# Linear attention and a soft tree on one core: the order of the fills, the residual in quarters, and where normalising, the state and the output's norm stand on VectorE

## The chip, the cores and the metric

The kernel runs on one core of a Trainium2 chip. The metric is the device time of one execution in microseconds (us), the median of the runs. TensorE, VectorE, ScalarE, GpSimd (POOL in the profile) and SyncE (SP) each work through a list of instructions of their own and meet only at semaphores.

## What is computed

x is [4, 2048, 256] in f32. Each row is normalised, xn = (x - mean)/sqrt(var + 1e-5), and the output is x + attention(xn) + tree(xn).

```python
# attention: 16 heads of 64
Q = phi(xn @ Wq + bq);  K = phi(xn @ Wk + bk);  V = xn @ Wv + bv      # phi(a) = elu(a) + 1
KV = KV + k_i v_i^T;  Ks = Ks + k_i                                   # token by token
o_i = (q_i KV) / (q_i Ks + 1e-6);   attention = o @ Wo + bo
# tree of depth 8
gate = sigmoid((xn @ tree_Wq^T) @ routers^T)
leaf_prob = product of gate or 1 - gate along each of 256 paths
tree = (leaf_prob @ leaf_values) @ Wout_w^T + Wout_b
```

## The kernel before

**Blocks, units, fills.** The 8192 tokens are worked in 16 blocks g of 512 (4 blocks a sequence), and a block in 8 units p, one for each pair of heads; n = 8g + p counts the units. The scan is done in chunks of 64 tokens. A unit has on TensorE first a *tiled* part (`tiled`, lines 974 to 994) of 64x64 matmuls: queries n on the state (`from_state`, in two passes), outer products of keys and values of unit n+1, queries on the state again, the scores of unit n+1 (line 893), then the chunk products of unit n with the masked scores (line 947). After it come the *fills*: each fill writes one bank of PSUM.

Matrix products in f32 are made of three passes over high and low halves, so a K, Q or V fill is six matmuls of 512 columns (`split_product`, line 806; the matmuls all have line 811). Unit n fills K of unit n+3, Q of unit n+2, and pieces of other work: V0 and V1 (values for heads 0 to 7 and 8 to 15, four chunks of 128 tokens each), xT (a transpose of the normalised x of block g+1), leaf (a transpose of the leaf probabilities), gate (the tree's gates of block g+1). The last unit of a block has oT (a transpose of the attention output) and y (the two output products, line 826).

**What sets the order.** `unit_fills` (lines 39 to 70) writes it by hand: K in bank W0, the "head" in S1, Q in S0, the "tail" in W1. All engines follow this one list; the banks S0 and S1 are also where the scores go. So a unit's scores wait (line 970 and 971) until the Q fill of the unit before has been converted and S0 and S1 are drained. `until_drained` in `outer_products` makes unit 0 wait for all four V0 chunks and unit 4 for all four V1 chunks.

In the loops over units each engine has a fixed sequence:

- ScalarE (lines 599 to 625): copies the scores out of PSUM (line 562, `copy_scores`), puts the transposed output of unit n-1 together (line 552), then for each fill relu and exp of K or Q (lines 522, 525), high halves of xT, leaf, oT (515, 545), tanh of the gates (530). The high half of the turned output (558) comes behind Q.
- VectorE (lines 765 to 794): `norm` (703 to 709: denominator, reciprocal, product) of unit n, `carry` (732: the running state, eight additions) of unit n+1, in unit 0 `normalise` (645) of the next block, then for each fill the drain: phi of K or Q (659), values (668), low halves (651, 683). `values_first` puts V ahead of Q in units 2 and 6 on VectorE alone. The low half of the turned output (697) comes last. `layer_norm` (632, 635) of block g+2 is in unit 7, and so are the outputs y (690).
- GpSimd (lines 478 to 504): the mask of the scores (406), the copy that takes the output apart into 16-bit planes (459), the copy that puts the turned keys together (467), the copy that takes the new keys apart (449), in unit 1 the `residual` (414: x plus bias into y_buf, for the whole block), in unit 7 the tree levels (422 to 439), and in unit 0 `inverse_deviation` (388, 390).
- SyncE: `turn_output` and `turn_keys` (DMA transpositions, lines 346 and 334), the stores of the block before in unit 0, and the load of block g+2 in unit 2, behind that unit's two transpositions.

TensorE's queue is kept short of waits: those that a unit needs are put ahead of the last matmul of a fill (`at_last`), where the matmuls before it still run: `head_ready` in K, `normed` (the output of unit n is out of PSUM) in Q, `masked` (the scores of n+1 are masked) in the last V.

## Time and profile before

| | us |
|---|---|
| median of 3 runs | 1218.85 (1218.16 to 1219.29) |
| the profiled execution, its own time | 1219.74 |
| its span (first to last instruction) | 1218.0 |
| TensorE matmuls busy | 1161.8 (95%) |
| VectorE busy | 836.1 (69%) |
| GpSimd busy | 804.3 (66%) |
| ScalarE busy | 681.0 (56%) |
| mean granted TensorE clock | 0.997 of full speed |

"Busy" is the time in which at least one instruction of the engine ran. A view of waits or of the timeline adds in brackets how long the engine had been idle ahead of an instruction and what released it. Matmuls overlap, so each is listed with more time than the distance to the next; distances are read from starts.

### The profile page before, as it was taken

What the parts mean: (1) busy time and instruction counts of PE and PEld (TensorE: products, weight loads), DVE (VectorE), ACT (ScalarE), POOL (GpSimd) and SP (SyncE); (2) the same over time, 40 slices, a digit from 0 to 9 for tenths busy, and PEclk for the clock granted to TensorE, in tenths of its full rate; (3) what the DMA queues carried; (4) which work ended last, traced back from release to release, by engine and by line L of the source; (5) the groups of instructions that cost most, each with busy time, mean ns of one, the idle gap of its engine ahead of it and who ended that gap; (6) DMA issues with size and microseconds to landing.
All of it is one profiled execution on the core that took longest, in us unless ns stands there. A gap on an engine that the chain in (4) does not pass through costs nothing.

```text
span 1218.0 us, 48108 instructions
## 1 busy us (share of the span) xinstructions
PE 1161.8 (95%) x21233; PEld 996.0 (82%) x21233; DVE 836.1 (69%) x2186; ACT 681.0 (56%) x990; POOL 804.3 (66%) x951
## 2 busy tenths in 40 slices
PE   5899999999999999999999999999999999999986
PEld 4789788887878879778897888878788797888866
DVE  4775875858677585876858667585876758767482
ACT  3563674737557374673737547374673746647371
POOL 3586667667666676766667676676666667676571
PEclk9999999999999999999999999999999999999998
DMA  7143532525344252533524435252452625335251
GB/s 233 20 80 52 86 68 54 91 52 89 60 65 90 45 97 50 89 63 55 93 49 90 58 62 98 45 89 54 84 68 57 94 45 89 63 57 77 55 71 36
DMA packets 271298, 87.54 MB, mean 72 GB/s; under 512 B 250721, under 2 KB 269424, under 8 KB 271088
## 3 DMA queue, kind: packets, MB, share of 16 engines
q1 hardware_dynamic: 271088, 84.46, 39.0%
q8 instruction: 166, 2.72, 1.0%
q14 instruction: 44, 0.36, 0.1%
HBM read 14.43 MB, written 8.39 MB: 19 GB/s over the span
## 4 chain that ended last, share of the span: by engine, by line
PE 63%; DVE 18%; ACT 6%; DMA 5%; issue 4%; POOL 3%; SPq 1%; POOLq 0%; ACTq 0%; DVEq 0%
PE w_pair L811 17%; PE s_pair L811 11%; PE s_pair L826 9%; PE o_pair L826 9%; PE s_pair L893 5%; PE o_pair L947 4%; DVE snaps L732 4%; DVE qT L659 3%; PE o_pair L933 3%; DVE oT L697 3%; DVE v_aug L668 3%; DVE xn L645 2%; DMA k_turned<-k_planes 2%; PE kv_pair L906 2%; ACT ex L522 2%
## 5 line engine op out<-in xcount | busy, mean ns | idle before, releaser
L406 POOL TENSOR_SCALAR_AFFINE_SELECT aT<-aT 64x512 f32<-64x512 f32 x256 | 171.7, 671 | 264.6 <-ACT aT L562 254.9
L562 ACT ACTIVATE aT<-s_pair 128x512 f32<-128x512 f32 x128 | 76.5, 598 | 382.6 <-PE s_pair L893 382.6
L811 PE MATMUL w_pair<-xnT,wk 128*128 128x512 f32 x768 | 212.1, 411 | 2.2 <-ACT k_tok L535 2.2
L811 PE MATMUL s_pair<-xnT,wq 128*128 128x512 f32 x756 | 201.1, 401 | 0.6 <-DVE o_tok L709 0.3
L732 DVE TENSOR_TENSOR snaps<-kv_pair,snaps 128x65 f32<-128x65 f32 x768 | 173.4, 226 | 26.4
L467 POOL COPY k_tok<-k_turned 128x1024 uint16<-128x1024 uint16 x126 | 171.4, 1361 | 22.7 <-POOL ffn_tok L459 14.6
L811 PE MATMUL w_pair<-wv,xnT 128*128 128x512 f32 x654 | 170.0, 395 | 0.0
L525 ACT ACTIVATE ex<-ex 128x512 f32<-128x512 f32 x256 | 161.9, 633 | 8.1
L449 POOL COPY k_planes<-kT 128x1024 uint16<-128x1024 uint16 x126 | 132.7, 1053 | 49.2 <-issue 26.5
L811 PEld LDWEIGHTS w_pair<-xnT,wk 128*128 128x128 f32 x768 | 134.3, 188 | 34.4 <-ACT k_tok L535 2.7
L811 PEld LDWEIGHTS s_pair<-xnT,wq 128*128 128x128 f32 x756 | 135.1, 188 | 27.0 <-DVE o_tok L709 2.4
L811 PEld LDWEIGHTS w_pair<-wv,xnT 128*128 128x128 f32 x654 | 122.8, 188 | 28.5
L659 DVE SCALAR_TENSOR_TENSOR qT<-s_pair,bias_one,ex 128x512 f32<-128x512 f32 x126 | 94.1, 747 | 61.2 <-ACT ex L525 61.2
L459 POOL COPY ffn_tok<-o_tok 128x1024 uint16<-128x1024 uint16 x109 | 113.5, 1041 | 7.6 <-DMA ffn_tok<-ffn_tok 0.8
L522 ACT ACTIVATE ex<-w_pair,neg_bias 128x512 f32<-128x512 f32 x130 | 89.6, 689 | 48.0 <-PE w_pair L811 47.2
L933 PE MATMUL o_pair<-snaps,qT 64*64 64x65 f32 x3584 | 113.5, 224 | 0.5 <-DVE state L732 0.4
L522 ACT ACTIVATE ex<-s_pair,neg_bias 128x512 f32<-128x512 f32 x126 | 86.8, 689 | 48.0 <-PE s_pair L811 47.6
L906 PE MATMUL kv_pair<-v_aug,k_tok 64*64 64x65 f32 x4096 | 92.1, 220 | 14.4 <-POOL k_tok L467 8.6
L697 DVE TENSOR_TENSOR oT<-o_full,oT 128x512 fp32r<-128x512 f32 x109 | 99.3, 911 | 3.0 <-ACT oT L558 3.0
L659 DVE SCALAR_TENSOR_TENSOR kT<-w_pair,bias_one,ex 128x512 f32<-128x512 f32 x128 | 95.2, 744 | 8.1 <-ACT ex L525 5.2
L826 PE MATMUL o_pair<-wo,oT 128*128 128x256 f32 x768 | 98.7, 283 | 1.8 <-DVE oT L697 1.8
L893 PE MATMUL s_pair<-qT,kT 64*64 64x64 f32 x4096 | 87.0, 221 | 12.2 <-DVE qT L659 9.0
(117 smaller groups left out, 2076.6 us busy)
## 6 DMA issues: line engine op xcount, KB each, us to landing
x_in<-in_L_attn_x_dram SPq DMA_DIRECT2D x16, 256.0 KB, 3.1
x_in<-in_L_attn_x_dram SPq DMA_DIRECT2D x32, 128.0 KB, 3.2
out_dram<-y_buf SPq DMA_DIRECT2D x32, 128.0 KB, 1.7
out_dram<-y_buf SPq DMA_DIRECT2D x64, 64.0 KB, 2.3
k_turned<-k_planes SPq DMA_TRANSPOSE x126, 3.2
stage<-in_L_attn_Wv_dram SPq DMA_DIRECT2D x2, 512.0 KB, 7.8
stage<-in_L_attn_Wk_dram SPq DMA_DIRECT2D x2, 512.0 KB, 10.0
stage<-in_L_attn_Wq_dram SPq DMA_DIRECT2D x2, 512.0 KB, 12.2
```

The lines of the kernel that those rows point to most:

```text
L406: pool.affine_select(out=part, in_=part, compare_op=ALU.is_ge, fill=0.0, base=0, pattern=[[0, 2 * CH], [1, D]], channel_multiplier=-1).the ...
L449: pool.tensor_copy(k_planes[:, :, :], kT[:, m % 2].bitcast(U16).rearrange("p (t s) -> p s t", s=2))\
L467: pool.tensor_copy(k_tok[:, :, :].rearrange("p c f -> p (c f)").bitcast(U16) .rearrange("p (n s) -> p s n", s=2), k_turned[:, :, :].rearra ...
L522: act.activation(ex[:, slot], psum_of(name), ACT.Relu, scale=-1.0, bias=neg_bias[:, col:col + 1])\
L525: act.activation(ex[:, slot], ex[:, slot], ACT.Exp, scale=-1.0).then_inc(exp_ready, 1)
L659: dve.scalar_tensor_tensor(out=dst, in0=psum_of(name), scalar=bias_one[:, col:col + 1], in1=ex[:, slot], op0=ALU.add, op1=ALU.max)\
L697: dve.tensor_tensor(oT[:, 1, p], o_full[:, 1, p], oT[:, 0, p].bitcast(F32), ALU.subtract)\
L732: dve.tensor_tensor(dst, added, so_far, ALU.add).then_inc(sum_ready, 1)
L811: last = pe.matmul(dst, l, r, start=i == 0, stop=i == len(steps) - 1)
L826: last = pe.matmul(dst[:, (c % 2) * hid:(c % 2 + 1) * hid], oT[:, a, t, tile_of_output(c)] if t < PAIRS else leafT[:, a, t - PAIRS, cols], ...
L893: last = pe.matmul(s_pair[rows_of(a), h, t * D:(t + 1) * D], kT[rows_of(h), p % 2, at], qT[rows_of(h), p % 2, at], start=True, stop=True)
L933: last = pe.matmul(output_at(t, h, a), qT[rows_of(h), p % 2, t * P + a * D:t * P + (a + 1) * D], before, start=turn == 0 and half not in b ...
```

## The change

- The fills of a unit become K, V, Q, and then what is left. V1's chunks 2 and 3 go from the tail to the head in units 1 and 2, V0's four chunks of the next block from the tail to the head in units 3 to 6; xT, leaf and gate go to the tail, behind Q.
- VectorE's order in a unit becomes: carry of unit n+1, norm of unit n, K, V, low half of the turned output, Q, tail. `values_first` goes. ScalarE's high half of the turned output comes right behind K.
- `normalise` of block g+2 stands in unit 7 of block g, behind `layer_norm`, instead of in unit 0 of block g+1; GpSimd's `inverse_deviation` for it goes between two tree levels. It has a new wait for the put-together outputs that lie in the same buffer.
- The residual is made in four parts, in units 1, 3, 4 and 5; the load of block g+2 moves from unit 2 to unit 6 on SyncE.
- TensorE's waits move: masks at the half of Q, norm at its last matmul, xT drained at the last matmul of K, the tail's needs at the last matmul of V.

```diff
@@ -42,19 +42,20 @@
     keys = divmod(n + 3, PAIRS) if n + 3 < blocks * PAIRS else None
     queries = divmod(n + 2, PAIRS) if n + 2 < blocks * PAIRS else None
     more = g + 1 < blocks
+
     head, tail = [], []
     if p == 0:
         head, tail = [("V1", 0, g)], [("V1", 1, g)]
     if p in (1, 2):
-        tail = [("V1", p + 1, g)]
+        head = [("V1", p + 1, g)]
         if more:
-            head = [("xT", p - 1, g + 1)]
+            tail = [("xT", p - 1, g + 1)]
+    if 3 <= p < PAIRS - 1 and more:
+        head = [("V0", p - 3, g + 1)]
     if p in (3, 4):
-        head = [("leaf", p - 3, g)]
-        if more:
-            tail = [("V0", p - 3, g + 1)]
+        tail = [("leaf", p - 3, g)]
     if p in (5, 6) and more:
-        head, tail = [("gate", p - 5, g + 1)], [("V0", p - 3, g + 1)]
+        tail = [("gate", p - 5, g + 1)]
     fills = [(("K", keys[1], keys[0]), W0)] if keys else []
@@ -363,8 +364,8 @@
                     turn_output(n)
                 if n + 3 < UNITS:
                     turn_keys(n + 3)
-                if p == 2 and g + 2 < BLOCKS:
-                    sp.wait_ge(x_consumed, g + 1)
+                if p == 6 and g + 2 < BLOCKS:
+                    sp.wait_ge(x_consumed, CH * (g + 1))
                     load_block(g + 2)
             store(BLOCKS - 1)
             sp.wait_ge(y_stored, STORES * BLOCKS)
@@ -407,13 +408,12 @@
                                        pattern=[[0, 2 * CH], [1, D]], channel_multiplier=-1).then_inc(a_masked, 1)
                 pool.wait_ge(a_masked, 2 * n + 2)
-            def residual(g):
+            def residual(g, c):
                 if g:
                     pool.wait_ge(y_stored, STORES * g)
                 pool.wait_ge(x_loaded[g % 2], LOADS * (g // 2 + 1))
-                pool.tensor_tensor(y_buf[:, :, :], x_in[:, g % 2],
-                                   y_bias[:, 0].unsqueeze(1).to_broadcast([P, CH, hid]), ALU.add)\
-                    .then_inc(x_consumed, 1)
+                pool.tensor_tensor(y_buf[:, c], x_in[:, g % 2, c], y_bias[:, 0], ALU.add).then_inc(x_consumed, 1)
+                pool.wait_ge(x_consumed, CH * g + c + 1)
             def gates(g):
                 for i in range(2):
@@ -438,6 +438,7 @@
                 pool.wait_ge(leaf_step, g * LEVEL_STEPS + 2 * l + 2)
                 pool.tensor_tensor(left, src[:, :, 0:n], right, ALU.subtract).then_inc(leaf_step, 1)
+            RESIDUAL_AT = (1, 3, 4, 5)
             FIRST_LEVELS = {0: range(0, 5), 1: range(5, 7), 2: range(7, depth)}
             def take_apart(m):
@@ -477,9 +478,9 @@
             take_apart(2)
             for n in range(UNITS):
                 g, p = divmod(n, PAIRS)
-                if p == 0 and g + 1 < BLOCKS:
-                    inverse_deviation(g + 1)
-                    pool.wait_ge(rstd_ready, 2 * g + 4)
+                if n == 0:
+                    inverse_deviation(1)
+                    pool.wait_ge(rstd_ready, 4)
                 if n + 1 < UNITS:
                     mask(n + 1)
                 if by_dma(n):
@@ -488,9 +489,8 @@
                     put_together(n + 2)
                 if n + 3 < UNITS:
                     take_apart(n + 3)
-                if p == 1:
-                    residual(g)
-                    pool.wait_ge(x_consumed, g + 1)
+                if p in RESIDUAL_AT:
+                    residual(g, RESIDUAL_AT.index(p))
                 if n in FIRST_LEVELS:
                     for l in FIRST_LEVELS[n]:
                         level(l, 0)
@@ -500,6 +500,10 @@
                     pool.wait_ge(o_turned_in, 16 * units_by_dma(n))
                     for l in range(depth):
+                        if l == 4 and g + 2 < BLOCKS:
+
+                            inverse_deviation(g + 2)
+                            pool.wait_ge(rstd_ready, 2 * g + 6)
                         level(l, g + 1)
                     pool.wait_ge(leaf_step, (g + 2) * LEVEL_STEPS)
@@ -605,15 +609,12 @@
                     put_output_together(n - 1)
                 for name, _ in unit_fills(n // PAIRS, n % PAIRS, BLOCKS):
                     kind, i, g = name
+                    if turned and kind != "K":
+                        high_of_turned(n - 1)
+                        turned = False
                     if kind in "KQ":
                         exponential(name)
-                        if kind == "Q" and turned:
-                            high_of_turned(n - 1)
-                            turned = False
                     elif kind == "oT":
-                        if turned:
-                            high_of_turned(n - 1)
-                            turned = False
                         high_of_output(name)
                     elif kind == "xT":
                         high(name, xnT[:, g % 2, 0, i])
@@ -641,6 +642,9 @@
                 if g == 1:
                     dve.wait_ge(filled[bank_of["tree", 1, 0]], count_of["tree", 1, 0])
+                if g > 1:
+
+                    dve.wait_ge(o_whole, units_by_dma((g - 1) * PAIRS - 2))
                 for c in range(CH):
                     last = dve.tensor_scalar(xn[:, c], x_in[:, g % 2, c], mean_var[:, c, 0:1], rstd[:, c:c + 1],
                                              ALU.subtract, ALU.mult)
@@ -669,14 +673,6 @@
                                   bv_all[:, half * n:(half + 1) * n].rearrange("p (h e) -> p h e", e=D), ALU.add)\
                    .then_inc(drained[bank_of[name]], 1)
-            def values_first(fills, p):
-
-                if p not in (2, PAIRS - 2):
-                    return fills
-                return [f for f in fills if f[0] not in ("Q", "V0", "V1", "oT", "kT")] + \
-                    [f for f in fills if f[0] in ("V0", "V1")] + \
-                    [f for f in fills if f[0] in ("Q", "oT", "kT")]
-
             def low_of_output(name):
                 _, p, g = name
                 dve.wait_ge(oT_hi, g * PAIRS + p + 1)
@@ -685,7 +681,7 @@
             def output(name):
                 i = name[1]
-                dve.wait_ge(x_consumed, name[2] + 1)
+                dve.wait_ge(x_consumed, CH * (name[2] + 1))
                 dve.wait_ge(filled[bank_of[name]], count_of[name])
                 dve.tensor_tensor(y_buf[:, 2 * i:2 * i + 2], psum_of(name).rearrange("p (c d) -> p c d", d=hid),
                                   y_buf[:, 2 * i:2 * i + 2], ALU.add)\
@@ -764,24 +760,24 @@
             for n in range(UNITS):
                 g, p = divmod(n, PAIRS)
-                norm(n)
                 if n + 1 < UNITS:
                     carry(n + 1)
-                if p == 0 and g + 1 < BLOCKS:
-                    normalise(g + 1)
-                fills = [name for name, _ in unit_fills(g, p, BLOCKS)]
+                norm(n)
+                if n == 0:
+                    normalise(1)
                 turned = n and by_dma(n - 1)
-                for name in values_first(fills, p):
+                for name, _ in unit_fills(g, p, BLOCKS):
                     kind, i, b = name
+                    if turned and kind not in ("K", "V0", "V1"):
+                        low_of_turned(n - 1)
+                        turned = False
                     if kind in "KQ":
                         phi(name)
                     elif kind == "oT":
-                        if turned:
-                            low_of_turned(n - 1)
-                            turned = False
                         low_of_output(name)
                         if p == PAIRS - 1 and g + 2 < BLOCKS:
                             layer_norm(g + 2)
+                            normalise(g + 2)
                     elif kind in ("V0", "V1"):
                         values(name)
                     elif kind == "xT":
@@ -803,9 +799,11 @@
                     waited[id(signal)] = count
                     pe.wait_ge(signal, count)
-            def split_product(dst, lhs, rhs, tiles, at_last=None):
+            def split_product(dst, lhs, rhs, tiles, at_half=None, at_last=None):
                 steps = [s for t in range(tiles) for s in passes(lambda a, t=t: lhs(a, t), lambda a, t=t: rhs(a, t))]
                 for i, (l, r) in enumerate(steps):
+                    if at_half and i == len(steps) // 2:
+                        at_half()
                     if at_last and i == len(steps) - 1:
                         at_last()
                     last = pe.matmul(dst, l, r, start=i == 0, stop=i == len(steps) - 1)
@@ -834,7 +832,7 @@
                 at = c % 2 * (CH // 2) + c // 2
                 return slice(at * P, (at + 1) * P)
-            def fill(name, at_last=None):
+            def fill(name, at_half=None, at_last=None):
                 kind, i, g = name
                 bank, dst = bank_of[name], psum_of(name)
@@ -843,11 +841,11 @@
                 if kind in "KQ":
                     wt = wk if kind == "K" else wq
                     last = split_product(dst, lambda a, t: wt[:, a, t, i * P:(i + 1) * P],
-                                         lambda a, t: xnT[:, g % 2, a, t], KT_, at_last)
+                                         lambda a, t: xnT[:, g % 2, a, t], KT_, at_half, at_last)
                 elif kind in ("V0", "V1"):
                     half, n = int(kind[1]), 2 * HALF * D
                     last = split_product(dst, lambda a, t: xnT[:, g % 2, a, t, i * P:(i + 1) * P],
-                                         lambda a, t: wv[:, a, t, half * n:(half + 1) * n], KT_, at_last)
+                                         lambda a, t: wv[:, a, t, half * n:(half + 1) * n], KT_, at_half, at_last)
                 elif kind in ("xT", "leaf"):
                     src = xn if kind == "xT" else leaf_even
                     for c in range(CH):
@@ -1051,13 +1049,18 @@
                 def normed():
                     until(o_normed, n + 1)
-                def head_ready():
-
+                def tail_ready():
                     for kind, i, g in (f for f, _ in fills):
                         if kind == "xT":
                             until(xn_ready, g + 1)
-                        if kind == "leaf" and i == 0:
+                        if kind == "leaf":
                             until(leaf_step, (g + 1) * LEVEL_STEPS)
+
+                def inputs_ready():
+                    for kind, i, g in (f for f, _ in fills):
+                        if kind == "V0" and i == 0:
+                            for t in range(KT_):
+                                until_drained(("xT", t, g))
                 def masked():
                     if n + 1 < UNITS:
@@ -1069,18 +1072,20 @@
                         until(s_copied, n + 2)
                     if kind in ("oT", "y"):
                         normed()
-                    if kind == "V0" and i == 0:
-                        for t in range(KT_):
-                            until_drained(("xT", t, g))
                     if kind == "leaf":
-                        until(leaf_step, (g + 1) * LEVEL_STEPS)
+                        tail_ready()
                     if kind == "y" and i == 0:
                         for t in range(LT):
                             until_drained(("leaf", t, g))
-                    fill(name, head_ready if kind == "K" else normed if kind == "Q" else masked if bank == W1 and kind in ("V0", "V1") else None)
-                    if kind == "y" and i == 0:
-                        masked()
+                    if kind == "K":
+                        fill(name, at_last=inputs_ready)
+                    elif kind == "Q":
+                        fill(name, masked, normed)
+                    elif kind in ("V0", "V1"):
+                        fill(name, at_last=tail_ready)
+                    else:
+                        fill(name)
                 normed()
                 masked()
```

## Rows read from the trace of the kernel before

**Rows 1.** The page, busy time, share of the span and instructions.

```profile
PE 1161.8 (95%) x21233; PEld 996.0 (82%) x21233; DVE 836.1 (69%) x2186; ACT 681.0 (56%) x990; POOL 804.3 (66%) x951
```

**Rows 2.** Timeline, ScalarE, line 562: start, duration (us), instruction, idle time and its releaser.

```profile
120.53 0.60 ACT L562 ACTIVATE aT<-s_pair 128x512 f32<-128x512 f32 x1 [13.73 <-PE s_pair L893]
...
413.49 0.60 ACT L562 ACTIVATE aT<-s_pair 128x512 f32<-128x512 f32 x1 [13.74 <-PE s_pair L893]
421.95 0.60 ACT L562 ACTIVATE aT<-s_pair 128x512 f32<-128x512 f32 x1 [2.30 <-PE s_pair L893]
428.79 0.60 ACT L562 ACTIVATE aT<-s_pair 128x512 f32<-128x512 f32 x1 [1.11 <-PE s_pair L893]
437.03 0.60 ACT L562 ACTIVATE aT<-s_pair 128x512 f32<-128x512 f32 x1 [2.52 <-PE s_pair L893]
...
450.71 0.60 ACT L562 ACTIVATE aT<-s_pair 128x512 f32<-128x512 f32 x1 [1.11 <-PE s_pair L893]
458.48 0.60 ACT L562 ACTIVATE aT<-s_pair 128x512 f32<-128x512 f32 x1 [1.11 <-PE s_pair L893]
466.82 0.60 ACT L562 ACTIVATE aT<-s_pair 128x512 f32<-128x512 f32 x1 [1.69 <-PE s_pair L893]
486.32 0.60 ACT L562 ACTIVATE aT<-s_pair 128x512 f32<-128x512 f32 x1 [13.74 <-PE s_pair L893]
...
1148.66 0.60 ACT L562 ACTIVATE aT<-s_pair 128x512 f32<-128x512 f32 x1 [14.61 <-PE s_pair L893]
1156.46 0.60 ACT L562 ACTIVATE aT<-s_pair 128x512 f32<-128x512 f32 x1 [1.63 <-PE s_pair L893]
```

**Rows 3.** Timeline, VectorE, block 5, unit 0: normalising.

```profile
416.96 2.26 DVE L645 TENSOR_SCALAR xn<-x_in,mean_var,rstd 128x256 f32<-128x256 f32 x4
```

**Rows 4.** Timeline, block 5, start of unit 3: the last V1 chunk and TensorE.

```profile
434.88 0.68 DVE L668 TENSOR_TENSOR v_aug<-w_pair,bv_all 128x512 f32<-128x512 f32 x1
435.61 0.34 PE L906 MATMUL kv_pair<-v_aug,k_tok 64*64 64x65 f32 x8 [0.51 <-DVE v_aug L668]
```

**Rows 5.** Residual and low half, block 5, unit 2; then line 697 alone: min/median/max ns.

```profile
427.79 2.38 POOL L414 TENSOR_TENSOR y_buf<-x_in,y_bias 128x1024 f32<-128x1024 f32 x1
428.45 2.26 DVE L697 TENSOR_TENSOR oT<-o_full,oT 128x512 fp32r<-128x512 f32 x1
...
L697 DVE TENSOR_TENSOR oT<-o_full,oT x109: 678/682/2827, 84.6 to 1200.5; 128x512 fp32r<-128x512 f32 x109
```

**Rows 6.** Timeline, TensorE, block 5, unit 0: outer products, scores, Q fill.

```profile
412.08 0.65 PE L906 MATMUL kv_pair<-v_aug,k_tok 64*64 64x65 f32 x32
412.78 0.65 PE L893 MATMUL s_pair<-qT,kT 64*64 64x64 f32 x32
...
416.72 1.55 PE L811 MATMUL s_pair<-xnT,wq 128*128 128x512 f32 x6
```

**Rows 7.** Timeline, block 15, units 4 to 5: Q filled last, then the scores.

```profile
1180.22 1.08 PE L811 MATMUL s_pair<-xnT,wq 128*128 128x512 f32 x4
...
1181.34 0.69 ACT L522 ACTIVATE ex<-s_pair,neg_bias 128x512 f32<-128x512 f32 x1
1182.72 0.75 DVE L659 SCALAR_TENSOR_TENSOR qT<-s_pair,bias_one,ex 128x512 f32<-128x512 f32 x1 [0.48 <-ACT ex L525]
...
1183.53 0.69 PE L893 MATMUL s_pair<-qT,kT 64*64 64x64 f32 x32 [0.44 <-DVE qT L659]
```

**Rows 8.** Timeline, VectorE, block 5, unit 0: first of norm, first of carry.

```profile
413.96 0.17 DVE L703 TENSOR_SCALAR den<-o_pair 128x8 f32<-128x8 f32 x1 [1.29 <-PE o_pair L947]
...
415.01 0.22 DVE L732 TENSOR_TENSOR snaps<-kv_pair,state 128x65 f32<-128x65 f32 x1
```

**Rows 9.** The page, groups: count, busy us, mean ns, idle us before and releaser.

```profile
L467 POOL COPY k_tok<-k_turned 128x1024 uint16<-128x1024 uint16 x126 | 171.4, 1361 | 22.7 <-POOL ffn_tok L459 14.6
...
L449 POOL COPY k_planes<-kT 128x1024 uint16<-128x1024 uint16 x126 | 132.7, 1053 | 49.2 <-issue 26.5
```

**Rows 10.** The page, DMA issues: count, size, median us from issue to landing.

```profile
x_in<-in_L_attn_x_dram SPq DMA_DIRECT2D x32, 128.0 KB, 3.2
```

## The prediction

> **What bounds the kernel now.** I read the page first: TensorE is busy for 1161.8 of 1218.0 us [rows 1], so time goes only where TensorE works or waits, and a gain must be a wait taken away. Next I read the copies of the scores on ScalarE (line 562). Each starts 0.71 us after TensorE's scores begin, so they are a clock of the units. In block 5 [rows 2] the copies are 8.46, 6.84, 8.24, 13.68 (two of 6.84), 7.77, 8.34 and 19.50 us apart, for units p = 0 to 7: 72.83 in all. I count each interval from the scores inside unit p to those inside unit p+1, and it holds p's fills. The mean over blocks 1 to 14 is (1148.66 - 120.53)/14 = 73.44 [rows 2].
>
> What would be the length without waits? Units 1 to 4 hold the same fills (K, Q, V and a transpose) and three of them take 6.84, so 2 is 1.40 too long. Units 5 and 6 hold K, Q, V and gate: 7.77 against 8.34, 0.57 too long. Unit 0 takes 7.80 in the last block (1148.66 to 1156.46), where nothing is normalised, against 8.46: 0.66 too long. 7.80 + 4 x 6.84 + 2 x 7.77 + 19.50 = 70.20. So block 5 waits 2.63 us and the mean block 3.24 us; over 15 blocks some 48 us, 4% of the span, is all that an order of work can win.
>
> The timeline names the causes. (a) Unit 0: VectorE spends 2.26 us on normalising at 416.96, its queue is late, and TensorE waits for Q [rows 3]. (b) Unit 2: the last V1 chunk is filled last, is drained at 434.88 to 435.56, and the outer products of the next unit wait 0.51 us for it; that V is also ahead of Q on VectorE [rows 4]. (c) Unit 6 the same with V0 of the next block. (d) In unit 2 the residual also holds GpSimd for 2.38 us from 427.79; VectorE's low half of the turned output starts at 428.45 and takes 2.26 us instead of 0.68, ending 0.54 after the residual does [rows 5].
>
> **What the change costs and gives.** *Removed.* V goes ahead of Q, so the last V1 or V0 is drained most of a unit before its outer products: (b) and (c) go. Normalising goes to unit 7 of the block before, where TensorE has 19.50 us of its own work: (a) goes. The residual in quarters is about 2.38/4 = 0.6 us a piece (a fixed part would make it more; 0.74 would still fit) and no longer holds VectorE for long: (d) goes. I count all 3.24 us of a mean block as won. If a third of what the mean has over block 5 (0.61) stays, it is 0.2 us a block.
>
> *Added: Q is late.* This is the step that decides. At present in units 1 to 4 a V fill follows Q before TensorE comes to the next scores. In the changed kernel only a transpose of four matmuls does. The scores need Q converted: ScalarE's two passes and VectorE's one. The length of that loop stands in the trace. Unit 0 already has the order K, V, Q: scores start at 412.78, Q's last matmul ends at 416.72 + 1.55 = 418.27, which is 5.49 us [rows 6]. From the end of Q to the scores that wait for it: in the last block Q is filled right before the next unit. It ends at 1180.22 + 1.08 = 1181.30, ScalarE begins at 1181.34, VectorE's pass ends at 1183.47, and the scores start at 1183.53 after an idle time put down to it: 2.23 us [rows 7]. The loop is 5.49 + 2.23 = 7.72, and 0.04 more because scores that have waited take 0.69 instead of 0.65: 7.76. TensorE's own work is 6.84. So each interval of units 1 to 4 grows to 7.76, a new wait of 0.92 (0.88 without the slower restart). Units 0, 5 and 6 have 1.4 us of fill behind Q both before and after: 7.80 and 7.77, just above the loop.
>
> A mean block becomes 7.80 + 4 x 7.76 + 2 x 7.77 + 19.50 = 73.88 against 73.44: +0.44, times 14 = **+6.2 us**.
>
> *Block 0.* Units 3 and 4 gain a wait of 0.92 each, unit 6 gives 0.57 back. In units 1 and 2 the output is transposed by TensorE on S1, and its low half now stands behind the transpose of x on both ScalarE and VectorE; nothing shows this order. It lies between nothing and about 1 us a unit (a ScalarE and a VectorE pass of some 0.5 each more); I take 1, since no fill is left behind it to cover it. Sum 1.84 - 0.57 + 2 = **+3.3** (1.3 at the low end). *Last block.* There is no V0, x or gate, so Q stands directly before the next unit in units 1 and 2: about 1 us each lost; in the last units carry is started without waiting for the end of the chunk products, which gives about as much back. I take 0, from -2 to +2.
>
> *State before output on VectorE.* Carry takes 416.96 - 415.01 = 1.95 us and norm 415.01 - 413.96 = 1.05 [rows 3, 8]. Carry needs only the outer products and both state passes, so it starts earlier, but the output is normed 1.95 - 0.9 = about 1.1 us later in an open unit. Behind it stand GpSimd's three copies: of the output, of the turned keys (1.36) and of the new keys (1.05) [rows 9]. From the scores' start in a 7.76 us unit I get carry at 0.5, norm 2.4 to 3.5, output copy 3.6 to 4.7, turned keys 4.75 to 6.1. TensorE comes to the next outer products 0.92 + 0.70 before the next scores (0.70 is 412.08 to 412.78 [rows 6]), at 6.14, so they may slip by 0.1 or 0.2. The new wait stands behind them and hides it: nothing. If that cover were gone, it would be at most 0.2 in four units, 12 us over 15 blocks.
>
> *Low half of the turned output.* It is moved from behind Q and V, where GpSimd was idle, to between V and Q. I put its start at 5.4 in the loop (K's pass at 4.15, V's at 4.8), into the copy of the turned keys. By the residual row it ends 0.54 after that copy, at 6.65. Q's own pass is due at 7.76 - 0.81 = 6.95. So it is hidden, with 0.3 to spare; see rival two.
>
> *Moved in queues.* SyncE loads x in unit 6 rather than 2, behind that unit's key transposition; no output transposition follows in unit 7, where the output goes through TensorE. Layer norm comes some 8 us into unit 7 and the load lands 3.2 us after its issue [rows 10]: hidden. If that cover were gone, the output of y on VectorE would slip, and it has several us. GpSimd's two rstd steps move between the tree levels of the same unit, and normalising on VectorE follows them: both end inside the 19.50 us. The waits inside Q (masks at its half, norm at its last matmul) are met 0.8 and 1.4 us before: nothing, or at most 0.3 in a unit or two of block 0.
>
> **Sum.** 6.2 + 3.3 + 0 = 9.5. The profiled execution took 1219.74 (span 1218.0 and 1.7 around it), so the changed one takes 1229.2. The median of the three runs is 1218.85, 0.9 lower, and I give **1228.3 us**. Its own bounds: with 0.88 for the wait, -2 in the last block and 1.3 for block 0 about 1222, with a stray wait of 0.2 kept and 2 in the last block about 1234.
>
> **Rival one, faster: Q is hardly late.** The place is the wait of the scores in units 2 to 5. The waits of now are all gone (-48 us), and the new one costs 60 x 0.92. If it were 0.16 less, at 0.76, the time would be that of before; at 0.4 it would be 1197, at nothing 1173. For it: VectorE's idle time grows, and only one row measures the 2.23. Against it: each step in that loop already starts 0.04 us after the one ahead, on idle engines; nothing is left to shorten. 19%, most of it near the point of no change.
>
> **Rival two, slower by more: VectorE and GpSimd shut each other out.** The low half reads two operands in SBUF. If it comes 0.7 us later than I put it, it finds the turned-keys copy done and the new-keys copy (1.05) begun. It then ends near 7.75, and Q's pass is 0.8 late. That costs 12 us if it falls in one unit of each block (1240), 48 in four (1276). For it: the residual row. Against it: 0.3 us of slack at the place where I put it. 14%. The Trainium skill (SBUF — State Buffer, Who interferes with whom) has such a rule and it speaks against this change: a VectorE instruction with both inputs in SBUF contends with a GpSimd instruction that reads SBUF, and the one issued first decides who blocks. By the residual row the trace agrees (2.26 us, ending with GpSimd's).
>
> **Rival three: the two sides cancel** within 0.2%. That bound, 2.4 us, is about what a measurement of this kernel can tell from no change. It needs a wait near 0.76, or a last block that wins 2 us and a block 0 that costs nothing. 12%.
>
> **Numbers.** The forecast has 55%. Slower 0.55 + 0.14 = 0.69, same 0.12, faster 0.19. The range goes down to 1212, where the wait is 0.65, and up to 1243, past the first price of rival two; 1173 and 1276 stay outside.
>
> **What would show it.** The copies of the scores in a middle block should stand 7.8, 7.76 (four times), 7.77, 7.77 and 19.5 apart. The wait of the scores for VectorE's Q pass should be by far TensorE's longest, in four units of every block, and the waits of outer products for V should be gone. Normalising should stand in unit 7 and the residual row at 0.6 to 0.74. I am wrong if the intervals of units 1 to 4 stay at 6.84 (rival one), or if those of 5 and 6 rise above 7.8 with low halves of over 1.3 us (rival two).

## The result and the profile after

The changed kernel takes **1232.26 us** (median of 4 runs, 1232.01 to 1234.57), against 1218.57 for the kernel before on the same chip: ratio 1.0116, interval 1.0098 to 1.0133. That is slower by 13.7 us where 9.5 was forecast. It is inside the range; the median lies 4.0 us above the predicted 1228.3. The profiled execution is the slowest of the four (1234.57, span 1232.9).

First the page of the changed kernel, the busy times and the shares of the chain that ended last:

```profile
PE 1157.0 (94%) x21233; PEld 1005.7 (82%) x21233; DVE 858.4 (70%) x2186; ACT 680.3 (55%) x990; POOL 829.1 (67%) x999
...
PE 82%; ACT 8%; DVE 7%; issue 1%; DMA 1%; SPq 0%; POOL 0%; POOLq 0%; DVEq 0%; ACTq 0%
```

TensorE has as many instructions as in [rows 1] and is busy 4.8 us less in a span that is 14.9 longer: the loss is waiting. Where it waits is in the timeline of ScalarE, the copies of the scores of block 5 (now line 566; columns as in [rows 2]):

```profile
422.29 0.60 ACT L566 ACTIVATE aT<-s_pair 128x512 f32<-128x512 f32 x1 [13.85 <-PE s_pair L891]
430.09 0.60 ACT L566 ACTIVATE aT<-s_pair 128x512 f32<-128x512 f32 x1 [1.63 <-PE s_pair L891]
437.87 0.60 ACT L566 ACTIVATE aT<-s_pair 128x512 f32<-128x512 f32 x1 [1.11 <-PE s_pair L891]
445.62 0.60 ACT L566 ACTIVATE aT<-s_pair 128x512 f32<-128x512 f32 x1 [1.11 <-PE s_pair L891]
453.39 0.60 ACT L566 ACTIVATE aT<-s_pair 128x512 f32<-128x512 f32 x1 [1.11 <-PE s_pair L891]
461.16 0.60 ACT L566 ACTIVATE aT<-s_pair 128x512 f32<-128x512 f32 x1 [1.11 <-PE s_pair L891]
```

They stand 7.80, 7.78, 7.75, 7.77 and 7.77 us apart: the unevenness of before has gone, and so have its short intervals of 6.84. The waits of TensorE, summed over the span, first three lines of before and then two of after (us in total, times, longest):

```profile
PE s_pair L893 <- DVE qT L659: 9.0, 17, 1.3
PE kv_pair L906 <- POOL k_tok L467: 8.6, 14, 1.1
...
PE kv_pair L906 <- DVE v_aug L668: 4.7, 10, 0.5
```

```profile
PE s_pair L891 <- DVE qT L663: 42.0, 64, 1.1
...
PE kv_pair L904 <- POOL k_tok L468: 3.8, 4, 2.1
```

64 waits of the scores for the converted Q: the four units a block that the forecast named, in 16 blocks (63 of them; one more falls in unit 0 of block 0). The waits of outer products for V are gone from the list. The trace of before also shows what block 5 alone did not: behind unit 2 of blocks 1 to 14 the outer products waited for V in ten blocks (4.7 us) and for the turned keys in ten (5.8 us).

The same count of intervals, as a mean over blocks 1 to 14, serves for all kernels of this study. I read it from the starts of the copies of the scores; "block" is the mean distance from the first copy of a block to the first of the next.

| kernel | units 0, 1, 2, 3, 4, 5, 6 | unit 7 | block |
|---|---|---|---|
| before | 8.47 6.85 8.32 6.84 7.09 7.78 8.35 | 19.74 | 73.44 |
| after | 7.80 7.78 7.77 7.77 7.77 7.78 7.78 | 19.50 | 73.95 |
| e1 without the fills | 7.80 6.86 7.51 7.12 7.26 7.79 8.34 | 20.28 | 72.96 |
| e2 no exp for Q | 7.80 7.24 7.33 7.42 7.39 7.78 7.78 | 19.49 | 72.22 |
| e3 Q before V | 7.78 6.97 7.71 7.18 7.42 7.75 7.74 | 20.10 | 72.66 |
| e4 V first where due | 7.80 7.80 7.77 7.83 7.84 7.80 7.78 | 19.52 | 74.13 |
| e5 and the turned halves last | 7.80 6.86 7.77 7.76 7.21 7.80 7.78 | 19.90 | 72.88 |
| e6 norm first | 7.80 7.78 7.77 7.77 7.77 7.78 7.78 | 19.37 | 73.82 |
| e7 V where due, norm first | 7.80 6.83 7.78 6.83 6.85 7.77 7.78 | 19.38 | 71.02 |
| e8 Q before V, norm first | 7.78 6.97 6.96 6.96 6.97 7.75 7.74 | 19.38 | 70.51 |
| e9 normalise sooner, alone | 7.80 6.84 8.21 6.83 6.89 7.77 8.34 | 19.74 | 72.43 |
| e10 residual in quarters, alone | 8.47 6.85 7.42 6.84 6.86 7.77 8.34 | 19.74 | 72.29 |
| e11 carry first, alone | 8.47 6.88 8.20 6.95 7.38 7.80 8.35 | 20.09 | 74.12 |
| e12 no exp, norm first | 7.80 7.12 7.10 7.11 7.10 7.78 7.77 | 19.38 | 71.17 |

The 14.9 us of the span are, after against before: start (to the copy of unit 1) 47.97 against 45.76, +2.2; block 0 78.70 against 74.77, +3.9; blocks 1 to 14 14 x 0.51 = +7.1; the last block, from its first copy to its last, 44.48 against 41.76, +2.7; what follows it -1.1. In every other kernel of the table the start took 44.9 to 46.3 (45.64 in e6, which differs from the changed kernel by one exchange on VectorE), so most of those 2.2 belong to the one execution that was profiled. The other terms give 12.7, near the 13.7 between the medians.

The loop itself, in the timeline of the changed kernel, block 5, unit 2, from one start of scores to the next:

```profile
437.11 0.69 PE L891 MATMUL s_pair<-qT,kT 64*64 64x64 f32 x32 [0.70 <-DVE qT L663]
...
439.95 0.69 DVE L705 TENSOR_TENSOR o_tok<-o_pair,rden 128x512 f32<-128x512 f32 x1
...
440.76 1.04 POOL L460 COPY ffn_tok<-o_tok 128x1024 uint16<-128x1024 uint16 x1 [0.79 <-POOL aT L407]
...
441.08 1.55 PE L809 MATMUL s_pair<-xnT,wq 128*128 128x512 f32 x6
...
441.86 1.35 POOL L468 COPY k_tok<-k_turned 128x1024 uint16<-128x1024 uint16 x1
...
442.53 1.17 DVE L693 TENSOR_TENSOR oT<-o_full,oT 128x512 fp32r<-128x512 f32 x1
442.67 0.69 ACT L526 ACTIVATE ex<-s_pair,neg_bias 128x512 f32<-128x512 f32 x1 [0.91 <-PE s_pair L809]
...
443.27 1.33 POOL L450 COPY k_planes<-kT 128x1024 uint16<-128x1024 uint16 x1
443.28 0.68 PE L904 MATMUL kv_pair<-v_aug,k_tok 64*64 64x65 f32 x32
443.38 0.63 ACT L529 ACTIVATE ex<-ex 128x512 f32<-128x512 f32 x1
...
444.05 0.75 DVE L663 SCALAR_TENSOR_TENSOR qT<-s_pair,bias_one,ex 128x512 f32<-128x512 f32 x1 [0.35 <-ACT ex L529]
...
444.85 0.69 PE L891 MATMUL s_pair<-qT,kT 64*64 64x64 f32 x32 [0.66 <-DVE qT L663]
```

From the scores' start: Q's last matmul ends at 5.52 (441.08 + 1.55), ScalarE works from 5.56 to 6.90, VectorE's Q pass runs from 6.94 to 7.69, scores at 7.74. The low half (line 693) starts at 5.42, takes 1.17 instead of 0.68 and ends at 6.59, 0.49 after the copy of the turned keys. So VectorE is idle for 0.35 us before the Q pass. The idle time listed for TensorE (0.66 to 0.70) is some 0.25 less than what the interval grew by (7.77 - 6.84 = 0.93): the matmuls ahead of it are listed with modelled ends. The weight loads (PEld in the views) list the same 64 waits with 50.9 us, 0.80 each. So a short delay can be missing from the matmuls' list; it is read from the weight loads' list and from the intervals.

### The profile page after: what moved, and what is told of

Same layout as the page of the kernel before. It is cut to its first block, busy times and chain, and to the rows that moved or that the text cites. A ratio compares the mean times of both kernels' runs of the same rounds, so it can differ in the third digit from the quotient of the medians.

```text
span 1232.9 us, 48202 instructions
## 1 busy us (share of the span) xinstructions
PE 1157.0 (94%) x21233; PEld 1005.7 (82%) x21233; DVE 858.4 (70%) x2186; ACT 680.3 (55%) x990; POOL 829.1 (67%) x999
## 4 chain that ended last, share of the span: by engine, by line
PE 82%; ACT 8%; DVE 7%; issue 1%; DMA 1%; SPq 0%; POOL 0%; POOLq 0%; DVEq 0%; ACTq 0%
PE s_pair L809 26%; PE w_pair L809 22%; PE s_pair L824 9%; PE o_pair L824 8%; PE s_pair L891 6%; PE o_pair L945 5%; DVE qT L663 4%; ACT ex L526 4%; ACT ex L529 4%; PE o_pair L931 3%; PE kv_pair L904 2%; DVE oT L693 1%; DMA ffn_tok<-in_L_ffn_Wout_w_dram 1%; PE w_pair L871 1%; DVE kT L663 0%
## 5 line engine op out<-in xcount | busy, mean ns | idle before, releaser
L407 POOL TENSOR_SCALAR_AFFINE_SELECT aT<-aT 64x512 f32<-64x512 f32 x256 | 168.1, 657 | 214.6 <-ACT aT L566 206.1
L809 PE MATMUL s_pair<-xnT,wq 128*128 128x512 f32 x756 | 196.6, 395 | 0.9 <-POOL aT L407 0.5
L450 POOL COPY k_planes<-kT 128x1024 uint16<-128x1024 uint16 x126 | 161.4, 1281 | 14.5 <-DVE kT L663 4.1
L809 PEld LDWEIGHTS s_pair<-xnT,wq 128*128 128x128 f32 x756 | 141.8, 188 | 35.6 <-POOL aT L407 1.7
L809 PE MATMUL s_pair<-wv,xnT 128*128 128x512 f32 x648 | 168.5, 395 | 0.0
L809 PEld LDWEIGHTS s_pair<-wv,xnT 128*128 128x128 f32 x648 | 121.6, 188 | 28.5
L693 DVE TENSOR_TENSOR oT<-o_full,oT 128x512 fp32r<-128x512 f32 x109 | 119.7, 1099 | 3.9 <-ACT oT L562 3.9
L891 PEld LDWEIGHTS s_pair<-qT,kT 64*64 64x64 f32 x4096 | 72.8, 135 | 53.3 <-DVE qT L663 50.9
## 6 DMA issues: line engine op xcount, KB each, us to landing
stage<-in_L_attn_Wk_dram SPq DMA_DIRECT2D x2, 512.0 KB, 10.3
```

What stands on the lines that cost most here:

```text
L407: pool.affine_select(out=part, in_=part, compare_op=ALU.is_ge, fill=0.0, base=0, pattern=[[0, 2 * CH], [1, D]], channel_multiplier=-1).the ...
L450: pool.tensor_copy(k_planes[:, :, :], kT[:, m % 2].bitcast(U16).rearrange("p (t s) -> p s t", s=2))\
L693: dve.tensor_tensor(oT[:, 1, p], o_full[:, 1, p], oT[:, 0, p].bitcast(F32), ALU.subtract)\
L809: last = pe.matmul(dst, l, r, start=i == 0, stop=i == len(steps) - 1)
L891: last = pe.matmul(s_pair[rows_of(a), h, t * D:(t + 1) * D], kT[rows_of(h), p % 2, at], qT[rows_of(h), p % 2, at], start=True, stop=True)
```

## The experiments

**The theory** for the loss: one loop through four engines (scores, K and V fills, Q, two ScalarE passes, VectorE's pass, scores), 7.76 us long, holds units 1 to 4, and everything else is below it. **The rivals**: that the norm behind carry, through GpSimd's copies and the outer products, or the low half that shares time with GpSimd, would hold the units nearly as long.

Each ratio below is to the kernel before, measured beside that run; the times come from several chips, so small differences between two of them mean little.

### e1: all but the order of the fills

The kernel before with its fills, `values_first`, TensorE's waits and turned halves as they were (the main lines of the edit; the load of x also moves to unit 6):

```diff
-                if p == 1:
-                    residual(g)
+                if p in RESIDUAL_AT:
+                    residual(g, RESIDUAL_AT.index(p))
...
-                norm(n)
                 if n + 1 < UNITS:
                     carry(n + 1)
-                if p == 0 and g + 1 < BLOCKS:
-                    normalise(g + 1)
+                norm(n)
...
                             layer_norm(g + 2)
+                            normalise(g + 2)
```

> The kernel before with three parts of the change (residual in quarters and x loaded in unit 6, normalising in unit 7, carry ahead of norm) and with the fills in their old order. Theory (what the change loses, it loses by the Q fill standing late; the other parts win): the interval of unit 0 falls from 8.47 to 7.80, unit 4's stray 0.25 goes, units 2 and 6 keep their waits for the last V (about 1.3 and 0.57), units 1, 3, 4 stay 6.84: about 72.2 a block, 1219 - 18 = 1201 us. Rival (carry ahead of norm, through the later output copy and turned keys on GpSimd, costs as much as the rest wins): units 1 to 4 come to over 7.0 each and the time to 1210 or more.

Measured: 1212.31, ratio 0.9937 (0.9913 to 0.996). The theory's 1201 was too low. The rival's mark for the time was met (over 1210), its mark for the units in three of four (6.86, 7.51, 7.12, 7.26). TensorE's waits:

```profile
PE kv_pair L911 <- POOL k_tok L467: 10.2, 24, 1.6
...
PE o_pair L831 <- DVE oT L701: 5.7, 14, 0.5
```

The outer products wait for the turned keys, because the norm is ready later, GpSimd's copy of the output waits for it, and the copy of the turned keys stands behind that. The second line is in unit 7, where the output product waits for the low half of the turned output; that unit grows from 19.74 to 20.28. So the other parts without the fill order win 7 us; the fill order and the place of the turned halves turn that into the loss of 14, a step of some 20 us.

### e9, e10, e11: the three parts one at a time

Each is one part of e1's edit on the kernel before: normalising in unit 7 (e9), the residual in quarters with the later load (e10; the two were not tried apart), carry ahead of norm (e11, whose whole edit follows).

```diff
-                norm(n)
                 if n + 1 < UNITS:
                     carry(n + 1)
+                norm(n)
```

> The kernel before with one part of the change: normalising (and GpSimd's two steps for it) in unit 7 of the block before. Theory: unit 0 goes from 8.47 to 7.80 and nothing else moves, 15 x 0.67 = 10 us less, about 1209. Rival (the wait of unit 0 moves on: with unit 0 shorter the residual and the output copy come later against unit 2): unit 2 grows by what unit 0 gives, 1215 or more.

> The kernel before with one part of the change: the residual in quarters and x loaded in unit 6. Theory (the whole residual held GpSimd for 2.4 us and through it VectorE's low half, the output copy and the turned keys): unit 2 goes from 8.32 to about 7.6, unit 4 from 7.09 to 6.85, about 15 us less, 1204. Rival (unit 2 waits for the last V alone): unit 2 stays above 8.1 and only the stray 0.25 of unit 4 goes, 1215.

> The kernel before with one part of the change: carry ahead of norm on VectorE. Theory (the norm is 0.9 us later, and with it the output copy, the turned keys and the next outer products, in units of 6.84): units 3 and 4 go up to 7.15, unit 2 by some, 0.3 to 1 us a block, 1224 to 1234. Rival (the state is what TensorE waits for, so that carrying it first wins): below 1216.

Measured: e9 1206.73, ratio 0.9882 (0.9862 to 0.9903); e10 1205.48, 0.9873 (0.9855 to 0.989); e11 1234.71, 1.0113 (1.0086 to 1.014). Two parts win 14 and 15 us, and the third loses 14. Added up they would win 15, and together in e1 they win 7: the late norm costs more once the other waits are gone.

e9 takes unit 0 from 8.47 to 7.80, unit 4 from 7.09 to 6.89 and unit 2 from 8.32 to 8.21. e10 takes unit 2 from 8.32 to 7.42 and unit 4 to 6.86. e11 shows what was hidden in the kernel after. Its timeline in unit 4 of block 5, from norm to the outer products:

```profile
450.99 0.69 DVE L709 TENSOR_TENSOR o_tok<-o_pair,rden 128x512 f32<-128x512 f32 x1
...
451.81 1.04 POOL L459 COPY ffn_tok<-o_tok 128x1024 uint16<-128x1024 uint16 x1 [1.14 <-issue]
...
452.91 1.36 POOL L467 COPY k_tok<-k_turned 128x1024 uint16<-128x1024 uint16 x1
...
454.32 0.70 PE L906 MATMUL kv_pair<-v_aug,k_tok 64*64 64x65 f32 x32 [0.16 <-POOL k_tok L467]
```

GpSimd stands idle for 1.14 us ahead of the output copy, though the mask is done, and from there the chain is back to back: norm, output copy, turned keys, outer products. Over the span these waits total 19.7 us in 31 places, against 8.6 in 14 before; unit 4 goes from 7.09 to 7.38. Half of the loss of a block (0.35 of 0.68) is in unit 7, 19.74 to 20.09. There the output product waits for the low half of the turned output, which stands behind the late norm on VectorE:

```profile
PE o_pair L826 <- DVE oT L697: 3.8, 9, 0.5
```

Before, it was 1.8 us in 4 places. The weight loads of that product wait 8.8 us for both low halves (lines 697 and 683), against 3.3 before: 5.5 us, near the 14 x 0.35 = 4.9 that unit 7 lost.

### e2: Q converted without its exponential pass

```diff
                 act.wait_ge(filled[bank_of[name]], count_of[name])
+                if kind == "Q":
+                    act.activation(ex[:, slot], psum_of(name), ACT.Relu, scale=-1.0, bias=neg_bias[:, col:col + 1])\
+                       .then_inc(exp_ready, 1)
+                    return
```

> The changed kernel; ScalarE leaves out the exponential pass of every Q fill (the relu pass stays), so Q's values are not phi(Q). Nothing else moves. Theory (the intervals of 7.77 in units 1 to 4 are the loop scores, K, V, Q, two ScalarE passes, VectorE's pass, scores): the loop loses 0.72 and these intervals become 7.05, four a block: 1232.3 - 15 x 4 x 0.72 = 1189 us; the copies of the scores show 7.05. Rival (GpSimd's copies or VectorE's total set the 7.77): the intervals stay above 7.5 and the time above 1216.

Measured: 1204.69, ratio 0.9873 (0.985 to 0.9896). Units 1 to 4 take 7.24 to 7.42: shorter, as the loop says, but not by the whole 0.72. The timeline in unit 4 of block 5 shows what came next:

```profile
444.95 1.35 POOL L469 COPY k_tok<-k_turned 128x1024 uint16<-128x1024 uint16 x1 [0.34 <-DMA k_turned<-k_planes]
445.36 1.43 DVE L698 TENSOR_TENSOR oT<-o_full,oT 128x512 fp32r<-128x512 f32 x1
446.36 0.69 PE L909 MATMUL kv_pair<-v_aug,k_tok 64*64 64x65 f32 x32
446.71 0.74 DVE L668 SCALAR_TENSOR_TENSOR qT<-s_pair,bias_one,ex 128x512 f32<-128x512 f32 x1
447.50 0.69 PE L896 MATMUL s_pair<-qT,kT 64*64 64x64 f32 x32 [0.22 <-DVE qT L668]
```

ScalarE's one pass over Q had ended at 446.18, but the Q pass on VectorE starts only with the end of the low half (445.36 + 1.43 = 446.79). The low half is now the last to be ready.

### e12: the same, with the turned halves last and norm first

The main lines of the edit (ScalarE's high half goes behind Q's pass as well):

```diff
+                norm(n)
                 if n + 1 < UNITS:
                     carry(n + 1)
-                norm(n)
...
                 for name, _ in unit_fills(g, p, BLOCKS):
                     kind, i, b = name
-                    if turned and kind not in ("K", "V0", "V1"):
-                        low_of_turned(n - 1)
-                        turned = False
```

> e2 (the changed kernel, the exponential pass of every Q fill left out) with the halves of the turned output last in the unit and norm ahead of carry. Theory (in e2 the loop was 7.05 and what held it at 7.25 to 7.4 was VectorE's low half behind GpSimd's copy and the late copies): all of units 1 to 4 at 7.05 to 7.1, about 1193 us. Rival (7.25 is the loop and the pass is worth less than 0.72): the intervals stay at 7.25.

Measured: 1189.13, ratio 0.9736 (0.9716 to 0.9756), units 1 to 4 at 7.10 to 7.12. Without the two other limits the loop is shorter by 7.77 - 7.11 = 0.66, near the pass taken out (0.63 and the 0.04 to its next; the 0.72 of e2's expectation was a little too much). So the loop is shown by its length with a piece removed. Which of the two limits mattered more in e2 is not separated, since e12 takes both away. The matmuls' list has almost no wait for the loop (2 of the scores for the Q pass, 0.9 us), though the units are still 0.27 longer than 6.84. The weight loads' list has it, 60 times: four in each of blocks 1 to 14, and four more:

```profile
PEld s_pair L899 <- DVE qT L671: 11.5, 60, 0.6
```

### e6: norm ahead of carry in the kernel after

```diff
-    if n + 1 < UNITS:
-        carry(n + 1)
     norm(n)
+    if n + 1 < UNITS:
+        carry(n + 1)
```

> The changed kernel with one exchange on VectorE: norm ahead of carry, as before the change. Theory (in the changed kernel only the Q loop holds units 1 to 4; GpSimd's copies come 0.1 late but the wait for Q hides it): the intervals stay 7.77, the time within 3 us of 1232. Rival (the late norm is what makes the changed kernel slower): units 1 to 4 fall below 7.5 and the time below 1216.

Measured: 1231.01, ratio 1.0095 (1.0071 to 1.0119); every interval of units 0 to 6 as in the kernel after, and unit 7 19.37 instead of 19.50. What costs 14 us by itself (e11) costs next to nothing here: it lies under the wait for Q.

### e3: Q filled before V

```diff
     fills = [(("K", keys[1], keys[0]), W0)] if keys else []
-    fills += [(name, S1) for name in head]
     if queries:
         fills.append((("Q", queries[1], queries[0]), S0))
+    fills += [(name, S1) for name in head]
```

VectorE still drains V ahead of Q; the low half goes last. TensorE's waits for the masks and the norm move from Q's fill to V's.

> The changed kernel with one exchange in the list of fills: K, Q, V, tail instead of K, V, Q, tail. VectorE still drains V ahead of Q and takes the low half of the turned output last; ScalarE's high half is behind Q's passes. Theory (Q's place alone costs the 0.93): Q is converted 1.4 us earlier, V is drained just in time; units 1 to 4 fall to 6.85 to 7.0, the block to 70.4 to 71, the time to 1180 to 1190 us. Rival (the V-first order also carries the gain, so taking V later brings the waits of units 2 and 6 back): these two stay at 8.2 and 8.3, the block near 72.3, the time near 1207.

Measured: 1208.33, ratio 0.9908 (0.9887 to 0.9929). Q's wait is gone and unit 1 falls to 6.97, but units 2, 3 and 4 take 7.71, 7.18 and 7.42, and the outer products wait 42 times for the turned keys:

```profile
PE kv_pair L913 <- POOL k_tok L468: 19.7, 42, 1.2
```

This is e11's chain, uncovered. The theory that the loop alone made the loss gave 1180 to 1190 and falls in that form.

### e4 and e5: V ahead only where it is due, and then the turned halves last

e4, in the kernel after (TensorE also waits at K's last matmul for what the transposes need); e5 adds the second edit, and the same on ScalarE for the high half:

```diff
+    if p in (1, 3, 4, 5):
+        head, tail = tail, head
```

```diff
                 for name, _ in unit_fills(g, p, BLOCKS):
                     kind, i, b = name
-                    if turned and kind not in ("K", "V0", "V1"):
-                        low_of_turned(n - 1)
-                        turned = False
```

> The changed kernel with V ahead of Q only in units 0, 2 and 6, where the next outer products need its last chunk; in units 1, 3, 4 and 5 the old fills (xT, leaf or gate between K and Q, V behind Q). Theory: intervals 7.80, 6.84, 7.77, 6.84, 6.84, 7.77, 7.77, 19.5 = 71.1 a block against 73.95: 1232.3 - 14 x 2.8 - 4 = 1189 us. Rival (the late norm behind carry holds open units too): 1, 3 and 4 at 7.1 or more and the time above 1200.

> e4 with both halves of the turned output where the kernel before has them (ScalarE's behind Q's passes, VectorE's low half last in the unit). Theory (in e4 VectorE's low half, standing ahead of Q, waited for GpSimd's copy of the turned keys and kept Q late also where V stood behind Q): units 3 and 4 fall from 7.9 to about 7.15, now set by the copy of the turned keys behind the late norm as in e1, unit 1 to 6.9, unit 2 stays 7.77, unit 7 goes back to about 20.3: 72.6 a block, about 1207 us. Rival (something else in the changed kernel holds every unit at 7.77 or more): no change, above 1225 us.

Measured: e4 1232.29, ratio 1.0106 (1.0084 to 1.0127): nothing gained, though in units 1, 3 and 4 Q has a V fill behind it again. e5 1214.15, 0.9956 (0.9941 to 0.9971, 10 runs). The timeline of e4, block 5, unit 3:

```profile
446.45 1.35 POOL L470 COPY k_tok<-k_turned 128x1024 uint16<-128x1024 uint16 x1
446.54 1.75 DVE L695 TENSOR_TENSOR oT<-o_full,oT 128x512 fp32r<-128x512 f32 x1
446.75 0.68 ACT L528 ACTIVATE ex<-s_pair,neg_bias 128x512 f32<-128x512 f32 x1
447.46 0.63 ACT L531 ACTIVATE ex<-ex 128x512 f32<-128x512 f32 x1
...
448.22 0.68 DVE L657 TENSOR_TENSOR leafT<-s_pair,leafT 128x512 fp32r<-128x512 f32 x1
448.82 0.74 DVE L665 SCALAR_TENSOR_TENSOR qT<-s_pair,bias_one,ex 128x512 f32<-128x512 f32 x1
...
449.61 0.58 PE L893 MATMUL s_pair<-qT,kT 64*64 64x64 f32 x24 [0.82 <-DVE qT L665]
```

Q's exponential ends at 448.09. The low half, started 0.09 us after GpSimd's copy, takes 1.75 us; the drain of leaf and the Q pass are queued behind it. So one Q that is on time is late again, and the unit is 7.8 long for another reason. e5 moves the low half behind them: units 1 and 4 go to 6.86 and 7.21, unit 3 stays at 7.76 and unit 7 rises to 19.90, with 37 waits for the turned keys (14.2 us). That is the norm's chain again. In unit 3 it holds TensorE twice: in blocks 1 to 14 the weight loads of Q's fill wait 7.9 us for the normed output (line 710) and those of the outer products 6.0 us for the turned keys, together 0.99 a block. That the unit comes out at 7.76, like the Q loop, is chance: no scores wait for Q at its end in those blocks. The expected 1207 us was missed because of this unit (7.15 was forecast).

### e7 and e8: the limits taken away together

e7 is e5 with norm ahead of carry; Q is still late in its unit 2. e8 is e3 with norm ahead of carry, and leaves none of the three limits. In both the turned halves go ahead of what follows K in unit 7 alone (the same on ScalarE for the high half):

```diff
+                    if turned and kind != "K" and p_last(n):
+                        low_of_turned(n - 1)
+                        turned = False
```

> e5 with norm ahead of carry, and with the turned halves ahead of Q in unit 7 alone. Theory (three limits, each now out of the way: Q late only in unit 2, low half last, copies early): 7.80, 6.84, 7.77, 6.84, 6.84, 7.77, 7.77, 19.4 = 71.1 a block, about 1184 us. Rival (VectorE itself is full in units of 6.84 once it also has V and the transposes): units 1, 3, 4 at 7.1 or more, 1195 or more.

> e3 (K, Q, V, tail) with norm ahead of carry, and with the turned halves ahead of Q in unit 7 alone. Theory (e3 was held by the copy of the turned keys at 7.2 and by V's drain in unit 2): units 1, 3, 4 at 6.95, unit 2 at 7.36, 5 and 6 at 7.75, 7 at 19.5: 71.1 a block, about 1185 us. Rival: units 3 and 4 stay at 7.2, the time above 1200.

Measured: e7 1187.97, ratio 0.9743 (0.9721 to 0.9765); e8 **1179.54**, ratio 0.967 (0.9645 to 0.9695). e8 computes everything and beats both kernels: 3.3% faster than before. Its timeline in unit 2 of block 5:

```profile
421.67 1.36 POOL L472 COPY k_tok<-k_turned 128x1024 uint16<-128x1024 uint16 x1
...
423.10 1.04 POOL L454 COPY k_planes<-kT 128x1024 uint16<-128x1024 uint16 x1
...
423.80 0.74 DVE L673 SCALAR_TENSOR_TENSOR qT<-s_pair,bias_one,ex 128x512 f32<-128x512 f32 x1
423.80 0.65 PE L923 MATMUL kv_pair<-v_aug,k_tok 64*64 64x65 f32 x32
...
424.60 0.62 PE L910 MATMUL s_pair<-qT,kT 64*64 64x64 f32 x25
```

The turned keys are ready 0.77 us before the outer products (421.67 + 1.36 = 423.03), Q's pass ends 0.06 before the scores, and neither group has a wait listed, of its matmuls or of its weight loads. The mean block is 70.51, where the working ahead of the prediction put a block without waits at 70.20.

## Why the prediction was right, point by point

**The new wait** was the deciding step, and it held to 0.02 us: 7.76 forecast from two places of the trace of before [rows 6, 7], 7.77 measured, in four units of each block, and 7.80, 7.77, 7.77 for the others. Since the loop contains only steps that each stood in a row, its sum could be made without a run. The restart of 0.04 is there too (0.69 for the scores).

**The waits taken away**: (a), (b), (c) and (d) are all gone from the changed kernel. e9 and e10 show that (a) and (d) do more than I gave them alone: each also shortens unit 4, where the mean block had 0.25 that block 5 did not show. In unit 2 the residual and the later load are worth 0.90 (8.32 to 7.42). The other 0.58 is put down to the last V: it is as much as in unit 6 (8.34 against 7.77), and the weight loads of e10 wait for V and then for Q in both units; no run takes it away alone. I had named both causes and not said how the 1.40 splits.

**The mean block**: +0.51 measured against +0.44. Unit 7 came as put, 19.50 (0.13 of it is the late norm: 19.37 in e6); the missing 0.07 is 0.01 to 0.02 in each of units 1 to 6, and 14 x 0.07 is 1.0 us.

**Block 0**: +3.9 against +3.3. The terms I named came out as named: units 1 and 2 +0.97 and +0.98 (1 each), 3 and 4 +0.94 and +0.92 (0.92 each), 6 -0.57. For units 1 and 2 no row gave a size, and I chose the upper end of 0 to 1; that it fitted so well is in part luck. The cause is as named: the weight loads of the scores wait 1.00 us there for the low half of the transposed output (line 679). Not named: unit 0, 10.29 against 9.48, +0.81; unit 7 gave back 0.12. The 0.81 can't be put down to the change: unit 0 of block 0 takes 9.1 to 9.7 in before, e1 to e4 and e12, and 10.3 to 10.7 in all others, e9, e10 and e11 among them, while e1, which has the parts of all three, takes 9.15. What decides between the two stays open.

**The last block** failed as a size, though inside its bounds: I took 0, from -2 to +2, and it is +2.7 to its last copy of the scores and -1.1 behind it, 1.6 in all. Of the 1 us lost in each of units 1 and 2, unit 1 lost 1.38 (6.39 to 7.77) and unit 2 nothing (7.83 to 7.77): it was already that long before, with the waits that the change takes away. The earlier carry does give something back, 1.1 us behind the last copy: the span goes on there for 25.5 to 27.2 us in kernels with carry first and for 27.6 to 28.9 with norm first. What I put at nothing is what the late norm takes just ahead of that. The last interval grows from 6.13 to 7.37, and its outer products wait 2.05 us for the turned keys instead of 0.75; with carry first alone (e11) it is 7.83.

**State before output**: the events came where I put them. Norm from 2.41 to 3.53 (2.4 to 3.5 forecast), output copy 3.65 to 4.69 (3.6 to 4.7), turned keys 4.75 to 6.10 (4.75 to 6.1), outer products at 6.17 (6.14). "Nothing, because the wait for Q hides it" holds (e6). But the price without the cover failed: I wrote at most 12 us, in four units, and e11 alone cost 14. The four units were not what was short: they lose 0.31 a block in e11 (0.8 was priced). Missing from the price were unit 7 (0.35 a block, the output product behind the low half), the same unit of block 0 (0.87) and the last block (+1.95 to its last copy). With Q on time the price is higher still: putting norm first, and the turned halves ahead of Q in unit 7, wins 29 us from e3 to e8 and 26 us from e5 to e7.

**The low half** ended at 6.59 (6.65 forecast), Q's pass was due at 6.94 (6.95), 0.35 to spare (0.3). Rival two did not occur in the kernel after, but its mechanism is real: the low half holds the units as soon as Q's loop is shorter (e2) or Q is on time (e4). The Trainium skill (SBUF — State Buffer, Who interferes with whom) says that a VectorE instruction with both inputs in SBUF contends with a GpSimd instruction that reads SBUF. The trace agrees: 1.17 us (the kernel after) and 1.75 (e4) instead of 0.68 beside a GpSimd copy, and 0.73 on the mean in e8, where 79 of 109 low halves start with no GpSimd instruction running.

**Rival one** (hardly late) is excluded by 64 waits of 0.66 us on the mean in the records; **rival three** by the interval. **The quarter residual** takes 0.73, the upper of the two values given, 64 times.

So the direction, the place and the size per unit were right, and of the 4.2 us missing between +9.5 and +13.7, 1.0 lie in the middle blocks, 0.6 in block 0 (less than the 0.81 of its unit 0, which belongs to no part of the change) and 1.6 in the last. The remaining 1.0 is of the size by which runs differ and stays open.

## What to carry to other kernels

Three loops of nearly one length held these units: Q's conversion (7.76), the low half behind a GpSimd copy (7.3 to 7.8 once it is last), and norm through GpSimd's copies to the outer products (7.1 to 7.7). Working on only one of them gained between next to nothing (e4, e6) and 28 us (e2, which leaves out a part of the computation), and taking away all gained 53 (e8 against after), so in a kernel tuned to such a balance write out each loop from start to start and mend them together. A fill that ends a loop (here Q) belongs as early as its inputs allow, with work that nobody waits for behind it; and a part that costs nothing under a wait may be the first thing to pay for when that wait goes (e6 against e11).

## What the runs showed of the hardware

Two things were not expected in their size. The contention works in both directions. In the changed kernel the GpSimd copy of the new keys takes 1.33 us on the mean in the 104 places where it starts while the low half still runs, and 1.04 in the other 22; the groups of the page, before in [rows 9] (1053 ns), after:

```profile
L450 POOL COPY k_planes<-kT 128x1024 uint16<-128x1024 uint16 x126 | 161.4, 1281 | 14.5 <-DVE kT L663 4.1 <-POOL k_tok L468 2.9
...
L693 DVE TENSOR_TENSOR oT<-o_full,oT 128x512 fp32r<-128x512 f32 x109 | 119.7, 1099 | 3.9 <-ACT oT L562 3.9
```

228 ns more a copy, 29 us of GpSimd time over 126 copies, beside a VectorE instruction that itself ends 0.49 us after the GpSimd copy that was running when it started. And a GpSimd instruction has a fixed part: four quarters of the residual take 4 x 0.73 = 2.92 us where the whole took 2.39, so some 0.18 us each ((2.92 - 2.39)/3). The split, with the later load of x, is still worth 15 us by itself (e10): the longest low half there takes 1.55 us instead of 2.83, and the waits of the outer products for the turned keys fall from 8.6 to 2.4 us.
